# Decoder kernel on one core: the second half's first attention step placed between the steps of the first half's feed-forward

## The chip, the core and the metric

The kernel runs on one core of a Trainium2 chip. The metric is the device time of one launch in microseconds (us). TensorE multiplies matrices and transposes tiles through a matrix unit; VectorE, ScalarE and GpSimd work on tiles of 128 partitions; SyncE issues the DMAs. Each engine carries out its own list of instructions in the order written, and waits on semaphores for the others.

## What is computed

The input is 16 sequences of 128 tokens with 128 features. The reference, cut to its outline:

```python
x = x + encoder(layernorm(x))              # 4 layers: linear attention, ReLU feed-forward
x = x + cross_attention(layernorm(x), ctx) # 16 heads, softmax, mask
x = x + bit_ffn(layernorm(x))              # quantized products, 3-tap convolution, SiLU
x = x + topk_attention(layernorm(x))       # 16 heads, the 64 highest scores of each row
x = x + channel_attention(layernorm(x), ctx)
x = x + experts(layernorm(x))              # 8 experts, SiLU(x Wg) * (x Wu), Wd

# encoder, one layer; elu(t) + 1 is computed as relu(t) + min(exp(t), 1)
# at the start: x = sqrt(128) * x_in + position
h = layernorm(x) * s1 + b1
q, k, v = h @ Wq + bq, h @ Wk + bk, h @ Wv + bv
qp, kp = elu(q) + 1, elu(k) + 1
kv, ksum = kp.T @ v, sum(kp)               # per head
x = x + ((qp @ kv) / (qp @ ksum + eps)) @ Wo + bo
x = x + relu((layernorm(x) * s2 + b2) @ W1 + bf1) @ W2 + bf2
```

## The kernel before, in words

The 16 sequences are two halves of eight; a half is two slots (s = 0, 1) of four sequences, each slot a tile of 128 x 512 fp32. The first half runs alone: the encoder (`encode_half`, a loop of four layers), then `cross_and_forward(0)`: cross attention in eight turns, the quantized feed-forward ("bitnet") and the projections of the top-k attention. Then `beside_encoder` merges the first half's top-k attention (turn b = one sequence) with the second half's encoder: the encoder is eight steps, step k being layer k // 2 of slot k % 2, and turn b holds attention of step b + 1, feed-forward of step b, and the head of step b + 2. Then come `cross_and_forward(1)`, in whose gaps the channel attention and first experts of the first half run (`beside(n)`), and the second half's top-k turns with all the expert products.

The order of the work is written by hand in each engine's block; there is no planner. Semaphores count events: `both(s, n)` and `nth(s, n)` give the count at which the n-th event of a slot has happened, so an event that changes its place in the order needs another count.

What the change touches, by the lines of the kernel before:

- Layer norm on VectorE: `layer_norm` (1874: four statistics, four aggregates), GpSimd's `ln_rsqrt` (633) or `step_rsqrt` (818), then `normalize` (1886) or `step_normalize` (2263), four `tensor_scalar`. `ln(n, update)` (1911) does it for both slots around an update.
- The feed-forward, `cross_and_forward`. On VectorE (2453): after the cross attention's loop of ten passes `crossed` (2512) adds the residual (`residual`, 1943) and quantizes (`quantize`, 2495); then four chunks c of 128 hidden features (2536): scale the product (2543), maxima of the chunk before (2534), two tap sums per slot (2551, 2553); then the second quantization (2556), `convolved` (2573) with the last norm LN_D, and `topk_values` (2587: centering of the keys, values). On ScalarE (1208): copies, tap activations (1233), SiLU (1238), copies (1244), `projected` (960). On TensorE (1787): transposes of the quantized tile (1802), a product with ones (1805), products `first(c)` (1807), transposes of a chunk (1827), the second product (1829 to 1844), `topk_projections` (1310).
- Banks of PSUM of those products: `FORWARD_BANKS` and `PROJECT_BANKS` (101, 102). In the first half slot 0 has banks 0 to 3 and slot 1 has 4 to 7; in the second half they have 0, 1 and 2, 3.
- Between `cross_and_forward(0)` and turn -1: the second half's input norms (2605 to 2612), `embed(1)` (2238: sqrt(128) x + position, then the norm of step 0's and step 1's attention), `attend(0, "input")` and `"projections"` on TensorE (1603), "input", "queries", "keys" on ScalarE (1103), "projections" on VectorE (2367), `spread_keys(0)` on GpSimd (860).
- `attend(k, part)`, one step's attention in parts: TensorE 1485 ("input": transposes; "projections": 1498, 1502; "sums": 1507; "attention": 1513; "attended": transposes; "output": 1523), VectorE 2270 ("projections" 2278, 2279; "queries" 2282; "keys" 2286; "sums" 2289, 2290; "attention" 2294 to 2298; "output" 2303 with `step_norm`), ScalarE 1032.
- `merged_turn(b)` for b from -1 to 9 in each block. Turn -1 has attention of step 0 (all parts behind the projections), the scores of sequence 0 (`scores`, 1397; 1408), their copies and signs on ScalarE (973, 985), and the head of step 1.
- `residual_base` (691) on GpSimd adds the bias and the normed tile to the residual of the first half, two sums per slot, right after the norms LN_D.

```python
# VectorE, chunk c of the feed-forward (lines 2536 to 2555, cut)
for s in SL:
    dve.wait_ge(c_f1_mm, nth(s, hf * CH + c + 1))
    dve.tensor_tensor(cbuf[s][:, :, 1:P + 1], bank4(FORWARD_BANKS[hf][s][2]),
                      rsb[s][:, :].rearrange("p (b t) -> p b t", b=G), ALU.mult).then_inc(c_deq, 1)
if c >= 1:
    for s in SL:
        chunk_max(s, c - 1)
for s in SL:
    dve.wait_ge(c_tap1, nth(s, hf * CH + c + 1))
    ...
if hf == 1:
    beside(1)
```

Of the kernel before, what the change touches and what calls it, by code (L numbers as in the profile page):

```python
# [27 lines left out]
P = 128  # L28
NSEQ = 16
SLOTS = 2  # L30
G = 4
# [69 lines left out]
FORWARD_BANKS = (((0, 1, 2, 3, 0, 1, 2), (4, 5, 6, 7, 4, 5, 6)), ((0, 1, 0, 1, 0, 1, 0), (2, 3, 2, 3, 2, 3, 2)))  # L101
PROJECT_BANKS = (((0, 2, 1, 3), (4, 6, 5, 7)), ((0, 1, 0, 1), (2, 3, 2, 3)))
# [22 lines left out]
NORM_AT, TURNED_AT = enc_orders()  # L125
NX_AT = {}
# [76 lines left out]
def decoder(nc, x, ctx, mask, aw, acolA, acolB, arow, w2a, bw, bcol, brow, cw, cconv, dw, dcol, drow,  # L203
            erow, ecol, mg, mu, md, ident_d, const_d, pos_d, out):
    stack = ExitStack()
    with stack:
# [173 lines left out]

        def xbank(g, k):
            return bank4(k)[:, 0:GROUPS[g][1], :]
# [72 lines left out]

        def norm_no(kind, k):

            done = 2 * NLN + 2 + NORM_AT[kind, k] + 1
            return done, done - 4

        def turned_no(kind, k):
            return 2 * (2 * NTR + TURNED_AT[kind, k] + 1)
# [145 lines left out]
        def _(pool):  # L608
# [24 lines left out]
            def ln_rsqrt(s, n):  # L633

                pool.wait_ge(ln_var, nth(s, n + 1))
                met(pool)
                pool.tensor_scalar(veps[s][:, :], mv[s][:, :, 1], EPS, None, ALU.add).then_inc(ln_veps, 1)  # L637
                pool.wait_ge(ln_veps, nth(s, n + 1))
# [52 lines left out]
            def residual_base(s, hf):  # L691
# [3 lines left out]
                pool.wait_ge(ln_h, both(s, hf * NLN + (LN_D + 1)))  # L695
# [134 lines left out]
            def merged_turn(b):  # L830
# [17 lines left out]
                if 0 <= b + 1 < STEPS:  # L848
                    attend_base(b + 1)
                if 0 <= b < STEPS:  # L850
                    step_rsqrt("A", b + 2)
                if 0 <= b + 1 < STEPS:
                    step_rsqrt("F", b + 1)
                if 0 <= b < NB:
                    maxima_in_parts(b)

            def beside_encoder():
                for s in SL:
                    step_rsqrt("A", s)
                spread_keys(0)  # L860
                for b in range(-1, NB + 2):
# [32 lines left out]
            def cross_and_forward(hf):  # L894
# [5 lines left out]
                for s in SL:  # L900
                    ln_rsqrt(s, n0 + LN_C)
                for s in SL:
                    ln_rsqrt(s, n0 + LN_D)
                for s in SL:
                    residual_base(s, hf)
                if hf + 1 < HALVES:
                    for s in SL:
                        ln_rsqrt(s, n0 + (NLN + LN_IN))
# [14 lines left out]
        def _(act):  # L923
            def hT_copy(s, m, k):

                act.wait_ge(hT_mm, both(s, m + 1))
# [105 lines left out]
            def attend(k, part):  # L1032
                s, i = k % 2, L + k // 2
                if part == "input":
                    act.wait_ge(wqkv_in, i * 48 + 48)
                    act.wait_ge(hT_mm, turned_no("A", k))
                    act.activation(hT[s][:, :], bank(6), ACT.Identity, bias=colA[:, 1:2], scale=colA[:, 0:1]).then_inc(hT_done, 2)
                if part == "queries":
                    act.wait_ge(q_mm, both(s, i + 1))
                    act.activation(qe[s][:, :], bank(5), ACT.Exp, bias=colA[:, 2:3])  # L1040
                    act.activation(qT_of[1][s][:, :], bank(5), ACT.Relu, bias=colA[:, 2:3]).then_inc(q_exp, 2)
                if part == "keys":
                    act.wait_ge(k_raw, both(s, i + 1))
                    act.activation(ke[s][:, :, :], kk[s][:, :, :], ACT.Exp).then_inc(k_exp, 2)
                    act.activation(kp[s], kk[s][:, :, :], ACT.Relu).then_inc(k_relu, 2)
                if part == "attended":
                    act.wait_ge(atT_mm, both(s, i + 1))
                    act.copy(atT[s][:, :], bank(5)).then_inc(atT_done, 2)
# [1647 lines left out]
```

## Time and profile before

| | |
|---|---|
| runs, median (lowest to highest) | 1449.4 us (1447.85 to 1454.92), 3 runs |
| the profiled execution | 1452.73 us, span 1450.9 us |
| TensorE busy | 1053.8 us, 73% of the span |
| VectorE busy | 998.0 us, 69% |
| ScalarE busy | 671.1 us, 46% |
| GpSimd busy | 491.9 us, 34% |
| mean granted TensorE clock | 0.819 of full |
| chain that ended last | TensorE 49%, VectorE 28%, ScalarE 7%, GpSimd 7%, issue 7% |

The span is the time from the first to the last instruction; the execution's own time lies 1.8 us above it. Busy shares are averages over stages that have different limits, so they say little of a change in one stage: that is read from the timeline of the stage. The chain is followed back from the last instruction, at each step to what released it. The rows below are whole lines of such views; PE is TensorE, DVE VectorE, ACT ScalarE, POOL GpSimd; in square brackets stands the idle time before an instruction and what ended it.

### The profile page before, as it was taken

How to read it: one execution, taken by the hardware profiler on the slowest of the kernel's cores; microseconds unless marked ns; L12 is line 12 of the kernel's file. 1: busy time of each engine (PE TensorE's matmuls, PEld its weight loads, DVE VectorE, ACT ScalarE, POOL GpSimd, SP SyncE). 2: the span in 40 equal slices, each digit the busy share in tenths (PEclk: the TensorE clock that was granted, in tenths of full speed). 3: DMA queues.
4: the chain of work that ended last, by engine and by line, in shares of the span. 5: the costliest groups of instructions: out<-in, count | busy, mean ns of one | idle time of the engine just before them, and what ended most of it. 6: DMA issues, size and time to landing. Idle time of an engine off the chain costs nothing.

```text
span 1450.9 us, 17892 instructions
## 1 busy us (share of the span) xinstructions
PE 1053.8 (73%) x5079; PEld 695.7 (48%) x5082; DVE 998.0 (69%) x3100; ACT 671.1 (46%) x1767; POOL 491.9 (34%) x474
## 2 busy tenths in 40 slices
PE   2877775655476818777676669868899883888999
PEld 1766652323344515554454334433344462666887
DVE  5666657878637778778887886753776858765332
ACT  1443436733156526666423654325776653533322
POOL 5233235601335404444524730043343423331100
PEclk9898976765677767888655889989998986899999
DMA  3000110000000000000001001201111120223344
GB/s 124 21 18 29 29 41 9 1 0 1 0 10 21 12 3 17 14 17 9 1 1 51 1 1 37 66 22 47 52 45 45 48 73 15 67 77 92 113 135 123
DMA packets 41106, 53.88 MB, mean 37 GB/s; under 512 B 6112, under 2 KB 20080, under 8 KB 41008
## 3 DMA queue, kind: packets, MB, share of 16 engines
q1 hardware_dynamic: 40336, 50.80, 11.5%
q0 software_dynamic: 672, 1.98, 0.4%
q8 instruction: 37, 0.61, 0.2%
q14 instruction: 61, 0.50, 0.1%
HBM read 51.71 MB, written 1.05 MB: 36 GB/s over the span
## 4 chain that ended last, share of the span: by engine, by line
PE 49%; DVE 28%; ACT 7%; POOL 7%; issue 7%; DVEq 1%; DMA 0%; another core or an unknown queue 0%; SPq 0%; POOLq 0%; ACTq 0%
PE psum L1679 7%; PE psum L1690 6%; PE psum L1665 6%; PE psum L1450 2%; PE psum L1426 2%; PE psum L1757 2%; PE psum L1268 2%; PE psum L1346 2%; PE psum L1544 2%; DVE h L1890 2%; PE psum L1408 2%; PE psum L1764 2%; POOL Wk L680 2%; PE psum L1498 2%; ACT far L995 2%
## 5 line engine op out<-in xcount | busy, mean ns | idle before, releaser
L2188 DVE TENSOR_TENSOR big<-psum,qe 128x512 f32<-128x512 f32 x106 | 72.8, 687 | 154.7 <-PE psum L1690 75.4
L1144 ACT ACTIVATE qe<-psum 128x512 f32<-128x512 f32 x106 | 62.3, 596 | 124.4 <-PE psum L1679 120.3
L1665 PE MATMUL psum<-big,wexp 128*128 128x256 f32 (+1 forms) x340 | 115.8, 455 | 0.0
L995 ACT ACTIVATE far<-far,half_far,fmul 128x128 bf16<-128x128 bf16 x256 | 102.9, 488 | 22.7 <-DVE hit L1963 22.7
L637 POOL TENSOR_SCALAR veps<-mv 128x4 f32<-128x4 f32 x34 | 8.4, 246 | 294.6 <-DVE mv L1883 294.6
L1976 DVE MAX8 near<-Wk 128x8 f32<-128x128 f32 x512 | 103.0, 275 | 0.0
L1268 PE MATMUL psum<-ident,h 128*128 128x128 f32 x172 | 37.9, 347 | 78.4 <-DVE h L1890 53.3
L735 POOL TENSOR_TENSOR Wk<-Wk,far 128x1024 f32<-128x1024 f32 x32 | 68.2, 2136 | 67.9 <-ACT far L995 67.9
L1890 DVE TENSOR_SCALAR h<-xs,mv,rstd 128x128 f32<-128x128 f32 x128 | 57.9, 553 | 41.1 <-POOL rstd L639 37.9
L1665 PEld LDWEIGHTS psum<-big,wexp 128*128 128x128 f32 x340 | 69.0, 203 | 30.1 <-issue 21.9
L1346 PE MATMUL psum<-ident,Wk 128*128 128x128 f32 x256 | 48.0, 355 | 47.1 <-POOL Wk L680 44.2
L1690 PE MATMUL psum<-xin,wexp 128*128 128x512 f32 x128 | 70.4, 633 | 15.1 <-DVE far L2188 9.9
L973 ACT ACTIVATE S<-psum,tiny 128x1024 f32<-128x1024 f32 x32 | 35.7, 1114 | 92.3 <-PE psum L1408 92.3
L1679 PE MATMUL psum<-xin,wexp 128*128 128x512 f32 x128 | 76.0, 679 | 2.5 <-DVE vaug L2599 1.6
L985 ACT ACTIVATE far<-S 128x128 bf16<-128x128 f32 x256 | 75.0, 296 | 0.3
L726 POOL TENSOR_TENSOR Wk<-S,ngr 128x2048 f32<-128x2048 f32 x16 | 58.1, 3630 | 39.1 <-DVE hit L1963 39.1
L1346 PEld LDWEIGHTS psum<-ident,Wk 128*128 128x128 f32 x256 | 38.0, 182 | 69.0 <-POOL Wk L680 42.5
L1268 PEld LDWEIGHTS psum<-ident,h 128*128 128x128 f32 x172 | 23.5, 171 | 97.9 <-DVE h L1890 47.5
L757 POOL TENSOR_SCALAR nparts<-nmax 128x16 bf16<-128x16 f32 x16 | 5.2, 326 | 189.2 <-DVE nmax L2060 189.2
L1986 DVE MATCH_REPLACE8 Wk<-near,Wk 128x128 f32<-128x128 f32 x256 | 67.1, 273 | 0.0
L1426 PE MATMUL psum<-ctxT,kT 32*128 32x512 f32 x128 | 49.0, 848 | 23.4 <-DVEq L2054 22.2
L948 ACT ACTIVATE Wk<-S,nsm 128x128 f32<-128x128 f32 x128 | 49.5, 389 | 11.9 <-DVE nsm L2480 11.9
(343 smaller groups left out, 2915.0 us busy)
## 6 DMA issues: line engine op xcount, KB each, us to landing
wexp<-in_mg SPq DMA_DIRECT2D x48, 256.0 KB, 2.7
wexp<-in_mu SPq DMA_DIRECT2D x48, 256.0 KB, 3.0
wexp<-in_md SPq DMA_DIRECT2D x48, 256.0 KB, 3.0
w<-in_aw SPq DMA_DIRECT2D x8, 256.0 KB, 2.9
w<-in_w2a SPq DMA_DIRECT2D x8, 256.0 KB, 2.6
wqkv<-in_aw SPq DMA_DIRECT2D x8, 192.0 KB, 2.2
ctxt<-in_ctx SPq DMA_DIRECT2D x5, 256.0 KB, 4.6
xin<-in_x SPq DMA_DIRECT2D x4, 256.0 KB, 3.0
```

Source lines behind the costliest of these rows:

```text
L735: pool.tensor_tensor(Wk[t][:, heads, :], Wk[t][:, heads, :], far[t][:, heads, :], ALU.subtract).then_inc(z_ready, 1)
L985: ins = act.activation(far[n % 2][:, hd, :], S[n % 3][:, hd, :], ACT.Sign, accum_out=cnt[n % 2][:, hd:hd + 1])
L995: ins = act.activation(far[t][:, hd, :], far[t][:, hd, :], ACT.Identity, bias=half_far[:, 0:1], scale=fmul[t][:, hd:hd + 1])
L1268: mm = pe.transpose(dst[:, b * P:(b + 1) * P], src[:, b, :], eye)
L1346: mm = pe.transpose(bank(4 + g % 2)[:, j * P:(j + 1) * P], E[a % 2][:, 4 * g + j, :], ident[:, :])
L1426: pe.matmul(bank(j), kT_of[g // 2][g % 2][rows, c * P:(c + 1) * P], qblk[a % 2][rows, :, :].rearrange("p i q -> p (i q)"), start=True, sto ...
L1665: mm = pe.matmul(bank(4)[:, 0:w], wd[l % 2][:, c + j, :], hid_of[k >= EARLY][k % CH][:, j * w:(j + 1) * w], start=first and j == 0, stop=l ...
L1679: mm = pe.matmul(bank(5 + k % 2)[:, j * w:(j + 1) * w], wg[l % 2][:, (c + j) * P:(c + j + 1) * P], hTm[g], start=True, stop=True)
L1690: mm = pe.matmul(bank(U_BANK[k])[:, j * w:(j + 1) * w], wu[l % 2][:, (c + j) * P:(c + j + 1) * P], hTm[g], start=True, stop=True)
L1890: ins = dve.tensor_scalar(h[s][:, b, :], src[:, b, :], mv[s][:, b, 0:1], rstd[s][:, b:b + 1], ALU.subtract, ALU.mult)
L1976: ins = dve.max(near[:, hd, rank:rank + 8], Wk[t][:, hd, :])
L2188: dve.tensor_tensor(hid_of[k >= EARLY][k % CH], bank(U_BANK[k]), sg_of[k >= EARLY][k % 2], ALU.mult).then_inc(hu_done, 1)
```

## The change

Three things. First, order: the second half's input norms go into the last passes of the first half's cross attention; its embedding, the norm of step 0 and the whole attention of step 0 go between the steps of the first half's feed-forward, the output sum of step 0 and the statistics of step 1's norm between the two slots' `topk_values`. Turn -1 keeps the scores of sequence 0, the head of step 1, and the last normalization of both; `residual_base` goes there too. Second, tiles: what step 0 needs and the feed-forward still uses lies in parts of two score tiles, S[1] and S[2]. Third, banks: the first half's feed-forward uses four banks (0 to 3), as the second half's does, so that step 0 has banks 5 to 7. The counts of the moved events come from three tables.

```diff
-FORWARD_BANKS = (((0, 1, 2, 3, 0, 1, 2), (4, 5, 6, 7, 4, 5, 6)), ((0, 1, 0, 1, 0, 1, 0), (2, 3, 2, 3, 2, 3, 2)))
-PROJECT_BANKS = (((0, 2, 1, 3), (4, 6, 5, 7)), ((0, 1, 0, 1), (2, 3, 2, 3)))
+FORWARD_BANKS = (((0, 1, 0, 1, 0, 1, 0), (2, 3, 2, 3, 2, 3, 2)),) * HALVES
+PROJECT_BANKS = (((0, 1, 0, 1), (2, 3, 2, 3)),) * HALVES
...
+NORMS_MOVED = {e: 2 * LN_B + 3 + j for j, e in enumerate(
+    ((0, NLN + LN_IN), (1, NLN + LN_IN), (0, LN_C), (0, NLN + LN_A), (1, LN_C), (0, LN_D), (1, LN_D), (1, NLN + LN_A)))}
...
+        first_h = [S[1][:, 0:4, :], S[1][:, 4:8, :]]
+        first_kp, first_kk, first_ke = S[1][:, 8:12, :], S[2][:, 8:12, :], S[2][:, 12:16, :]
+        first_hT, first_qe = flat(S[2][:, 0:4, :]), flat(S[2][:, 4:8, :])
...
@@ GpSimd, merged_turn @@
-                if 0 <= b + 1 < STEPS:
+                if 1 <= b + 1 < STEPS:
                     attend_base(b + 1)
...
+                if b == -1:
+                    pool.wait_ge(ln_h, 2 * norm_no("F", 0)[0])
+                    for s in SL:
+                        residual_base(s, 0)
@@ GpSimd, beside_encoder @@
-                for s in SL:
-                    step_rsqrt("A", s)
                 spread_keys(0)
+                step_rsqrt("A", 1)
@@ GpSimd, cross_and_forward @@
+                if hf == 0:
+                    for s in SL:
+                        ln_rsqrt(s, NLN + LN_IN)
+                    ln_rsqrt(0, LN_C)
+                    ln_rsqrt(0, NLN + LN_A)
+                    ln_rsqrt(1, LN_C)
+                    pool.wait_ge(c_q1, 2)
+                    attend_base(0)
@@ ScalarE, cross_and_forward @@
                     act.activation(rsb[s][:, :], bank(FORWARD_BANKS[hf][s][1]), ACT.Copy, scale=wscale[:, 0:1]).then_inc(c_rs, 1)
+                    if hf == 0 and s == 0:
+                        attend(0, "input")
...
+                    if hf == 0 and c == 0:
+                        attend(0, "queries")
+                        attend(0, "keys")
                     for s in SL:
                         if hf == 1:
                             beside(1)
...
+                if hf == 0:
+                    attend(0, "attended")
@@ TensorE, topk_projections @@
-                if hf == 1:
-                    pe.wait_ge(pk_done, nth(s, 2 * hf + 2))
+                pe.wait_ge(pk_done, nth(s, 2 * hf + 2))
@@ TensorE, beside_encoder @@
-                attend(0, "input")
-                attend(0, "projections")
                 for b in range(-1, NB + 2):
                     merged_turn(b)
+                    if b == -1:
+                        projections_out(1, 0)
@@ TensorE, cross_and_forward: after the product with ones of slot 0; after chunk c; after slot 0's second product @@
+                    if hf == 0 and s == 0:
+                        attend(0, "input")
+                        attend(0, "projections")
...
+                    elif c >= 1:
+                        attend(0, ("sums", "attention", "attended")[c - 1])
...
+                    elif s == 0:
+                        attend(0, "output")
@@ VectorE, step_normalize @@
+                if (kind, k) in (("A", 2), ("F", 1)):
+                    dve.wait_ge(base_done, 4)
@@ VectorE, cross_and_forward @@
+                    if hf == 0 and b == NB:
+                        input_norm(0)
...
+                        if hf == 0:
+                            input_norm(1)
+                if hf == 0:
+                    for s in SL:
+                        normalize(s, NLN + LN_IN, xin[s], first_h[s])
...
                         quantize(0)
                         if hf == 1:
                             beside(1)
+                        else:
+                            embedded_first(0)
+                            dve.wait_ge(x_upd, sum_no(0, NLN + LN_A))
+                            layer_norm(0, NLN + LN_A, xs_of[1][0])
                     residual(hf, s)
+                    if hf == 0 and s == 1:
+                        normalize(0, NLN + LN_A, xs_of[1][0], first_h[0])
...
                 quantize(1)
                 if hf == 1:
                     beside(3)
+                else:
+                    embedded_first(1)
+                    attend(0, "projections")
...
                     if hf == 1:
                         beside(1)
+                    elif c == 0:
+                        attend(0, "keys")
+                        attend(0, "queries")
+                    elif c < CH - 1:
+                        attend(0, ("sums", "attention")[c - 1])
...
-                for s in SL:
-                    topk_values(s)
-                if hf + 1 < HALVES:
-                    for s in SL:
-                        dve.wait_ge(x_in[s], hf * 16 + 32)
-                        layer_norm(s, n0 + (NLN + LN_IN), xin[s])
-                    for s in SL:
-                        dve.wait_ge(base_done, 2 * nth(s, hf + 1))
-                        dve.wait_ge(hT_mm, both(s, hf * NTR + (TR_D + 1)))
-                        normalize(s, n0 + (NLN + LN_IN), xin[s])
+                topk_values(0)
+                if hf == 0:
+                    dve.wait_ge(x_upd, sum_no(1, NLN + LN_A))
+                    step_norm("A", 1)
+                    attend(0, "output")
+                topk_values(1)
...
+            def embedded_first(s):
+                dve.wait_ge(ln_h, 2 * ln_no(s, NLN + LN_IN))
+                dve.scalar_tensor_tensor(xs_of[1][s][:, :, :], first_h[s], float(np.sqrt(P)), pos[:, :].unsqueeze(1).to_broadcast([P, G, P]),
+                                         ALU.mult, ALU.add).then_inc(x_upd, 2)
```

In `attend` of each engine, `of_step(k, first, usual)` picks the tile in S[1] or S[2] for step 0 and the slot's own tile otherwise, and step 0's pair of banks for "sums" and "attention" is 6, 7 instead of 3, 4. `merged_turn` starts its attention at step 1 (`step = 1 <= b + 1 < STEPS`).

## Rows read from the trace of the kernel before

**Rows 1.** Windows: us; PE, PEld, DVE, ACT, POOL busy; PEclk; DMA
```profile
299.00:370.00 71.00, 37.18 (x170) 21.33 (x169) 59.18 (x153) 22.96 (x36) 10.64 (x12) 0.62 0.00 0
...
370.00:402.00 32.00, 13.72 (x44) 10.38 (x46) 17.65 (x60) 4.95 (x7) 8.33 (x11) 0.60 0.00 1
...
402.00:423.00 21.00, 11.72 (x34) 6.61 (x35) 10.31 (x24) 12.94 (x46) 7.22 (x5) 0.66 0.05 16
...
560.00:600.00 40.00, 31.98 (x180) 22.48 (x180) 31.22 (x131) 25.15 (x73) 17.54 (x17) 0.83 0.08 24
```

**Rows 2.** Timeline of TensorE (PE): start, us, line, operation, [idle before]
```profile
330.10 1.11 PE L1268 MATMUL psum<-ident,kk 128*128 128x128 f32 x4 [0.34 <-DVE kk L2553]
...
367.45 1.05 PE L1287 MATMUL psum<-watt,hT 128*128 128x128 f32 x8
...
380.36 1.09 PE L1268 MATMUL psum<-ident,h 128*128 128x128 f32 x4 [11.85 <-DVE h L1890]
...
382.49 3.75 PE L1498 MATMUL psum<-wqkv,hT 128*128 128x256 f32 x8 [1.04 <-ACT hT L1037]
...
386.03 1.41 PE L1502 MATMUL psum<-hT,wqkv 128*128 128x512 f32 x2
...
390.65 2.10 PE L1507 MATMUL psum<-vv,big 128*128 128x130 f32 x8 [3.22 <-DVE big L2286]
...
393.76 2.26 PE L1513 MATMUL psum<-kvs,qT 128*128 128x144 f32 x8 [1.00 <-DVE kvs L2290]
...
399.80 2.04 PE L1523 MATMUL psum<-wo,hT 128*128 128x128 f32 x8 [0.82 <-ACT hT L1048]
...
401.77 2.08 PE L1408 MATMUL psum<-kblk,qT 32*128 32x512 f32 x4
...
434.25 1.13 PE L1408 MATMUL psum<-kblk,qT 32*128 32x512 f32 x4
```

**Rows 3.** Timeline of VectorE (DVE), first attention of the second half
```profile
387.28 0.68 DVE L2278 TENSOR_TENSOR kk<-psum,rowkv 128x512 f32<-128x512 f32 x1
...
392.80 0.69 DVE L2289 TENSOR_TENSOR kvs<-psum,consts 128x512 f32<-128x512 f32 x1 [1.59 <-PE psum L1507]
...
396.13 0.23 DVE L2294 TENSOR_SCALAR den<-psum 128x64 f32<-128x64 f32 x1 [2.51 <-PE psum L1513]
...
414.61 0.69 DVE L2278 TENSOR_TENSOR kk<-psum,rowkv 128x512 f32<-128x512 f32 x1 [7.86 <-PE psum L1498]
```

**Rows 4.** Timeline of VectorE, first half from the cross attention's end on
```profile
289.47 1.22 DVE L1929 TENSOR_REDUCE zden<-Wk 128x8 f32<-128x1024 f32 x1 [1.18 <-ACT Wk L951]
...
296.44 0.69 DVE L1938 TENSOR_TENSOR far<-psum,consts 128x512 f32<-128x512 f32 x1 [1.64 <-PE psum L1357]
...
299.77 0.69 DVE L1947 TENSOR_TENSOR xs<-psum,xb 128x512 f32<-128x512 f32 x1 [1.55 <-PE psum L1364]
...
319.95 1.29 DVE L2543 TENSOR_TENSOR cbuf<-psum,ke 128x512 f32<-128x512 f32 x2 [2.94 <-remote]
...
361.04 3.15 DVE L1890 TENSOR_SCALAR h<-xs,mv,rstd 128x128 f32<-128x128 f32 x4 [1.58 <-POOL rstd L639]
```

**Rows 5.** Timeline of VectorE, embedding norm of the second half
```profile
376.05 0.87 DVE L1878 BATCH_NORM_STATS2 stats<-xs 128x6 f32<-128x128 f32 x4
...
379.10 1.11 DVE L1890 TENSOR_SCALAR h<-xs,mv,rstd 128x128 f32<-128x128 f32 x4 [1.65 <-POOL rstd L824]
```

**Rows 6.** Timeline of ScalarE (ACT), around a table load
```profile
1055.20 1.28 ACT L1004 ACT_TABLE_LOAD   x1
...
1056.50 1.02 ACT L1004 ACTIVATE big<-psum 128x1024 f32<-128x1024 f32 x1
```

**Rows 7.** Timeline of GpSimd (POOL), the first residual sum
```profile
360.97 1.27 POOL L696 TENSOR_TENSOR xs<-xs,ratt 128x512 f32<-128x512 f32 x1
```

**Rows 8.** Windows of five us around the stretch without TensorE work
```profile
365.00:370.00 5.00, 2.88 (x12) 1.73 (x12) 4.46 (x14) 1.95 (x3) 2.33 (x2) 1.00 0.00 0
...
380.00:385.00 5.00, 3.60 (x10) 2.81 (x11) 3.24 (x12) 2.06 (x2) 2.48 (x4) 0.50 0.00 0
```

More of the change, by code:

```diff
@@ L454, in cols, with ln_no, sum_no, tr_no @@
             return slice(WU * (u % 2), WU * (u % 2 + 1))
+        def ln_no(s, n):
+            return NORMS_MOVED[s, n] if isinstance(n, int) and (s, n) in NORMS_MOVED else nth(s, n + 1)
+        def sum_no(s, n):
+            return SUMS_MOVED[s, n] if isinstance(n, int) and (s, n) in SUMS_MOVED else both(s, n - n // NLN)
+        def tr_no(s, m):
+            return TURNED_MOVED[s, m] if (s, m) in TURNED_MOVED else both(s, m + 1)
         def norm_no(kind, k):
             done = 2 * NLN + 2 + NORM_AT[kind, k] + 1
-            return done, done - 4
+            return NORMS_MOVED[0, NLN + LN_A] if (kind, k) == ("A", 0) else done, done - 4
         def turned_no(kind, k):
-            return 2 * (2 * NTR + TURNED_AT[kind, k] + 1)
+            return TURNED_MOVED["A", 0] if (kind, k) == ("A", 0) else 2 * (2 * NTR + TURNED_AT[kind, k] + 1)
         def up_no(k, c):
@@ L1102, in beside_encoder @@
             def beside_encoder():
-                for part in ("input", "queries", "keys"):
-                    attend(0, part)
                 for b in range(-1, NB + 2):
@@ L1490, in attend @@
                     if k == 1:
-                        pe.wait_ge(v_raw, both(0, i + 1))
-                    transposes(bank(6), h[s], ident[:, :], hT_mm, 2)
+                        pe.wait_ge(lin_done, both(0, i + 1))
+                    transposes(bank(6), h_of("A", k), ident[:, :], hT_mm, 2)
                 if part == "projections":
@@ L1555, in merged_turn @@
                 before, old, new = 0 <= b - 1 < NB, 0 <= b - 2 < NB, 0 <= b + 1 < NB
-                step, fed, after = 0 <= b + 1 < STEPS, 0 <= b < STEPS, 0 <= b + 2 < STEPS
+                step, fed, after = 1 <= b + 1 < STEPS, 0 <= b < STEPS, 0 <= b + 2 < STEPS
                 if b == 7:
@@ L2316, in merged_turn @@
                 here, before, old = 0 <= b < NB, 0 <= b - 1 < NB, 0 <= b - 2 < NB
-                step, fed, after = 0 <= b + 1 < STEPS, 0 <= b < STEPS, 0 <= b + 2 < STEPS
+                step, fed, after = 1 <= b + 1 < STEPS, 0 <= b < STEPS, 0 <= b + 2 < STEPS
                 if b == 7:
```

98 lines of the change are left out of this document (56 added, 42 removed).

## Prediction

> **What bounds the kernel now.** I read the stretches first [rows 1]: between 370 and 402 us TensorE works 13.72 of 32 us and VectorE 17.65, ScalarE 4.95; nobody is busy, so this stretch is a chain. The timelines show which: input norm, embedding norm, then attention step 0, each waiting on the one before. TensorE sat idle 11.85 us before the first transposes [rows 2], and VectorE waits 1.59 and 2.51 us for the first products [rows 3]. The stretch ahead, 299 to 370 us, is different: VectorE is busy 59.18 of 71 us, TensorE 37.18 [rows 1]; it is VectorE's. The change takes work out of a chain with little overlap and lays it into a stage that VectorE bounds. The question is what each laid-in part costs there, including the waits it makes VectorE stand through, for VectorE, ScalarE and TensorE all run their own list in order.
>
> A difference under 0.5% (7 us) is about what a measurement of this kernel cannot tell from no change.
>
> **What the edits cost inside the first half's tail.** All of it is counted as the delay of the last normalization of the half (slot 1, start 361.04 [rows 4]).
>
> 1. Input norms. Slot 0's statistics (about 1.4 us) go ahead of a sum that had waited 1.18 us for ScalarE, slot 1's into the 1.64 us that VectorE idles for TensorE's outputs [rows 4]: nothing, or 0.1. Without those two covers they cost 2.8. The two normalizations (4 x 0.28 us each, 2.2 together) get the 1.55 idle before the cross attention's residual sum [rows 4]: **+0.6**.
> 2. Behind slot 0's quantization come embedding 0 (0.7, as the other sums over 512 [rows 3]), its statistics (1.4), and its normalization (1.11). That last waits for GpSimd's rstd: from the start of the statistics to the normalization the same pattern takes 3.05 us [rows 5], that is 1.64 of waiting, of which slot 1's residual sum fills 0.7. So 0.7 + 1.4 + 0.9 + 1.1 = **+4.1**. GpSimd's five rsqrts stand in VectorE's new order, so none waits behind another.
> 3. TensorE gets slot 0's transposes and projections ahead of slot 1's quantized transposes. They take 1.09 + 3.75 + 1.4 us with a ScalarE copy of 0.8 between [rows 2], about 7.1 us from the end of embedding 0's normalization; VectorE needs 8.0 us from there: 3.05 and 1.1 for slot 1's norm [rows 5], 3.85 for its quantization, which ended 2.94 before 319.95 [rows 4]. So TensorE is free in time. VectorE's embedding 1 and two projection sums (0.68 each [rows 3]) are 2.0 us, and VectorE had those 2.94 us of idle before the first chunk: **0**. GpSimd's sum for the attention's base (1.3 us) runs beside them. Without this cover it would be 2; a faster TensorE may give back up to 0.9 of the idle.
> 4. After chunk 0: keys and queries, two sums of 0.68, need the ScalarE exponentials, which now stand behind the chunk's two tap activations and take 2.3 us; that adds 0.15 of waiting. The Silu's table load (1.28 us [rows 6]) now comes after them, and Silu and the next taps land 0.7 us before VectorE wants them: **+1.5**.
> 5. After chunk 1: "sums" on VectorE directly waits for TensorE, whose products stand behind the transposes of the chunk just ended (the pair takes 1.0 us to the next issue; slot 1's own start at 330.10 [rows 2]) and take 2.10 at the low clock, about half at the high one. Nothing is between: VectorE stands 3.1 us (low) or 2.2 (high), then works 0.8. **+3.5** (3.0 to 3.9).
> 6. After chunk 2: "attention" in the same way, transposes and then 2.26 us of products [rows 2]: stands 3.3 or 2.2, then 1.7 us (two small ones and one of 0.7). **+4.5** (3.9 to 5.0). Queued behind both waits are the next chunk's scaling and maxima, and behind them ScalarE's taps and TensorE's next transposes: the whole stage shifts.
> 7. TensorE's "output" (2.04 us [rows 2]) stands between slot 0's second product and slot 1's transposes, which were ready the moment that product ended, and slot 1's product met VectorE with 0.1 us to spare: **+1.4** (0.9 to 1.9).
> 8. Four banks: the banks are reused, and each reuse already has a wait that has ended by then; the one new wait (values for the keys' copy) 0 to 0.1 us.
>
> Sum: 0.6 + 4.1 + 0 + 1.5 + 3.5 + 4.5 + 1.4 = **15.6 us later** (13.1 to 16.9).
>
> **What it takes out behind that normalization.** Before, from its start (361.04) to the second slot's projection sums (414.61 [rows 3]) 53.6 us pass. After:
> - the normalization no longer has GpSimd's residual sums beside it: it took 3.15 us for four that take 1.11 elsewhere [rows 4, 5], while GpSimd ran its sum at 360.97 [rows 7]. Those sums are now in turn -1, where VectorE has little to do. The normalization then frees slot 1's transposes at about +1.2, but TensorE is at slot 0's values until +2.7.
> - slot 1's tail on TensorE runs from the normalization's end (361.04 + 3.15 [rows 4]) to 368.50 (its last products [rows 2]), 4.3 us, and the scores of turn -1 follow at once, at +7.1. Their spread keys need 1.1 us of GpSimd behind slot 0's centering and are early.
> - from the scores to the projection sums is 12.84 us at the low clock (401.77 to 414.61), 11.0 in turn 0, where the scores take 1.13 instead of 2.08 [rows 2]. I take 12: +19.1.
> - on VectorE in that time: values 0 (2.3), norm of embedding 1 (1.4), output sum and norm (2.1), values 1 (2.3, after TensorE), two normalizations (2.2): done at about +11.6, when slot 1's transposes can go; TensorE is ready for them at about +10.5 to +11. It fits, with up to 1 us lost in the bound.
> - GpSimd's four base sums (1.27 us each [rows 7]) then end near +17, before the signed scores of turn 0 are asked for (+21). No new DMA is issued; SyncE's weight loads wait for the same events, earlier.
>
> 53.6 - 19.1 = **34.5 us** (30.9 if slot 1's tail and the scores all run at the low clock, which adds 2.8 to the tail; 35.5 at the high one).
>
> Net 34.5 - 15.6 = **18.9 us less**. The profiled execution took 1452.7 us around its span of 1450.9, so it would be 1433.8; the median of the runs is 3.3 lower, 1449.4, and I give the forecast against that: **1430.5**. All terms at the low clock: 30.9 - 16.9 = 14.0; all at the high one: 35.5 - 13.1 = 22.4.
>
> **Two rules of the skill.** Behind the table load at 1055.20 (1.28 us) the Exp starts at 1056.50 [rows 6], so a load costs 1.3 us here. The Trainium skill, ScalarE: Activation LUTs, section "What ACT_TABLE_LOAD costs", has a drain of about as much again on each switch, 2.66 us in all. By that, point 4 would be 0.6 us dearer, 1.4 less 0.7 to spare; the trace does not show it.
> The clock was 0.50 of full from 380 to 385 us, after TensorE had done nothing for 10 us, and 1.00 from 365 to 370 us, after steady work [rows 8]. The Trainium skill, TensorE: Matmul & The Clock Gate, "What's actually happening", says that idling halves the clock and sustained work restores it. By that, the filled hole should leave turn -1 at 2.4 GHz; the trace agrees at those two places, and over the feed-forward stage, with TensorE at work on and off, it was 0.62 [rows 1].
>
> **The rivals.**
> - *Clock stays high* (10%): the hole was what halved the clock, and turn -1 and the inserted products all run at 2.4 GHz. Gain 22.4 and up to 4 more if the next turn's start profits: 1423 to 1427. For it: 0.66 in 402 to 423 against 0.83 in a later turn [rows 1]. Against: that later turn still has its drops.
> - *More standing than I see* (12%): VectorE, in order, meets waits I sized at nothing (points 1 and 3 uncovered, 4.8; slot 1's transposes late in turn -1, 2): gain 8 to 14, 1437 to 1441.
> - *Serial all the same* (6%, no difference): every inserted part costs its full chain, so the 32 us of 370 to 402 are all paid in the feed-forward stage, and only GpSimd's interference (2.0) and slot 1's tail beside the new work (3.3) are saved: 1444. For it: points 5 and 6 are of that kind. Against: projections, copies and exponentials, some 12 us of the chain, run beside VectorE's work; 11.85 of TensorE's idle is gone anyway.
> - *Slower* (4%): the clock of the merged turns. A turn of 40 us has TensorE busy 32 at clock 0.83 [rows 1]; about half of the chain is TensorE's, 19 us. Should the shifted start put its drops on the chain, each turn costs 19 x (0.83/c - 1): at 0.71 it is 3.2 us, 26 over eight turns, which is the point where 19 us of gain turn into 7 of loss; at 0.68 it is 34, 1464. Against: the turns' order of work is unchanged.
>
> Forecast 68%. Faster 90% (forecast, high clock, more standing), same 6%, slower 4%. The range takes all of the forecast's span, most of the high-clock case and most of the standing case: 1422 to 1440.
>
> **What would show it.** VectorE waits of 2.2 to 3.1 us before the masked sums and 2.2 to 3.3 before the denominators, now ahead of the last normalization; that normalization 15.6 us later and 1.1 us long for its four; the 11.85 us hole gone; scores of turn -1 some 18 us earlier; turn 0 and all after it merely shifted. Wrong if turns 0 to 7 change length by more than 1 us each, if the first chunk starts late, or if the scores wait for spread keys or for slot 0's values.

## The result and the profile after

The changed kernel takes 1426.61 us (median of 4 runs, 1424.53 to 1429.59), the kernel before in the same comparison 1450.77 us: ratio 0.9835, interval 0.9807 to 0.9864, about 24 us less. The forecast was 18.9 us less, 1430.5. The profiled execution took 1429.59 us around a span of 1427.8. Line numbers of the changed kernel differ: 1890 is now 1947, 1947 is 2004, 2543 is 2620, 1408 is 1451, 1843 is 1893, 1523 is 1567, 2278 is 2339.

Two executions do not reach the changed code at the same time, so the sections below are counted from an anchor that both kernels have ahead of the first changed instruction, a reduction of the cross attention (before, then after, VectorE's timelines):

```profile
267.81 1.21 DVE L1929 TENSOR_REDUCE zden<-Wk 128x8 f32<-128x1024 f32 x1
```
```profile
266.13 1.21 DVE L1986 TENSOR_REDUCE zden<-Wk 128x8 f32<-128x1024 f32 x1
```

1.68 us of the difference between the two spans is therefore there before anything is changed. The stretches of [rows 1] in the kernel after (windows, same columns):

```profile
299.00:370.00 71.00, 37.20 (x169) 25.55 (x170) 57.40 (x151) 22.86 (x36) 6.72 (x9) 0.62 0.00 0
370.00:402.00 32.00, 21.01 (x71) 12.09 (x72) 19.48 (x65) 18.57 (x55) 18.09 (x15) 0.79 0.04 11
402.00:423.00 21.00, 15.78 (x76) 10.59 (x76) 8.84 (x32) 14.08 (x50) 8.18 (x7) 0.84 0.02 7
```

The windows are fixed times, and the feed-forward stage now runs until 373 us (before: 361), so they do not hold the same code. VectorE is busy 57.40 of 71 us instead of 59.18, although attention work was laid into the stage: it now stands in new waits, which the timeline below shows. The chain of 370 to 402 is gone (TensorE 13.72 to 21.01 us busy, ScalarE 4.95 to 18.57). VectorE's timeline, which answers to [rows 3 to 5]:

```profile
299.29 0.68 DVE L2004 TENSOR_TENSOR xs<-psum,xb 128x512 f32<-128x512 f32 x1
...
311.55 1.11 DVE L1947 TENSOR_SCALAR S<-xs,mv,rstd 128x128 f32<-128x128 f32 x4 [1.01 <-POOL rstd L668]
...
322.23 1.28 DVE L2620 TENSOR_TENSOR cbuf<-psum,ke 128x512 f32<-128x512 f32 x2
328.00 1.28 DVE L2620 TENSOR_TENSOR cbuf<-psum,ke 128x512 f32<-128x512 f32 x2
336.30 0.69 DVE L2351 TENSOR_TENSOR kvs<-psum,consts 128x512 f32<-128x512 f32 x1 [2.94 <-PE psum L1551]
...
337.04 1.28 DVE L2620 TENSOR_TENSOR cbuf<-psum,ke 128x512 f32<-128x512 f32 x2
345.60 0.22 DVE L2356 TENSOR_SCALAR den<-psum 128x64 f32<-128x64 f32 x1 [3.20 <-PE psum L1557]
...
347.19 1.28 DVE L2620 TENSOR_TENSOR cbuf<-psum,ke 128x512 f32<-128x512 f32 x2
368.95 1.13 DVE L2662 SCALAR_TENSOR_TENSOR xs<-psum,deq,xs 128x128 f32<-128x128 f32 x4 [0.51 <-PE psum L1893]
...
373.09 1.11 DVE L1947 TENSOR_SCALAR h<-xs,mv,rstd 128x128 f32<-128x128 f32 x4 [1.58 <-POOL rstd L668]
...
389.85 0.69 DVE L2339 TENSOR_TENSOR kk<-psum,rowkv 128x512 f32<-128x512 f32 x1 [5.68 <-PE psum L1542]
```

The first chunk no longer has idle time ahead of it (2.94 us in the kernel before). The four chunks start at 322.23, 328.00, 337.04 and 347.19, that is 5.77, 9.04 and 10.15 us apart. Ahead of the third and fourth stand the forecast waits, 2.94 before the masked sums and 3.20 before the denominators; both sit in front of the next chunk's scaling in VectorE's list. The last normalization takes 1.11 us for its four, as forecast. TensorE's timeline from the last second products on, with [rows 2] for before:

```profile
361.26 1.89 PE L1893 MATMUL psum<-wcq,big 128*128 128x128 bf16 x16 [0.68 <-ACT big L1288]
362.95 2.02 PE L1567 MATMUL psum<-wo,S 128*128 128x128 f32 x8
...
367.85 1.07 PE L1893 MATMUL psum<-wcq,big 128*128 128x128 bf16 x16 [0.72 <-ACT big L1288]
...
374.25 0.66 PE L1312 MATMUL psum<-ident,h 128*128 128x128 f32 x4 [1.11 <-DVE h L1947]
...
378.63 1.13 PE L1451 MATMUL psum<-kblk,qT 32*128 32x512 f32 x4
...
383.20 0.66 PE L1312 MATMUL psum<-ident,S 128*128 128x128 f32 x4 [1.00 <-DVE S L2328]
```

The same product of sixteen takes 1.89 us in slot 0 and 1.07 in slot 1: between the two, the clock rose. It stayed up over slot 1's tail and the scores (windows of the kernel after, columns as in [rows 1]):

```profile
345.00:363.00 18.00, 7.44 (x48) 5.62 (x46) 16.32 (x35) 5.45 (x9) 0.00 (x0) 0.50 0.01 1
363.00:368.00 5.00, 4.03 (x29) 3.34 (x28) 3.24 (x16) 2.15 (x4) 1.27 (x2) 0.60 0.00 0
368.00:373.00 5.00, 4.27 (x32) 2.76 (x30) 2.82 (x14) 1.96 (x3) 1.22 (x2) 1.00 0.00 0
373.00:378.00 5.00, 3.16 (x14) 1.55 (x13) 4.70 (x20) 1.61 (x3) 1.09 (x2) 1.00 0.00 2
378.00:383.00 5.00, 2.89 (x15) 1.14 (x13) 4.75 (x20) 2.23 (x3) 4.04 (x5) 1.00 0.02 3
383.00:390.00 7.00, 4.70 (x13) 3.62 (x14) 1.32 (x6) 6.95 (x35) 5.02 (x4) 0.57 0.00 0
```

So TensorE had 2.4 GHz from 368 to 383, and 1.2 GHz from 345 to 363, where it was at work for 7.44 of 18 us. The Trainium skill, TensorE: Matmul & The Clock Gate, section "What's actually happening", has sustained work bring the full clock and idling take it away. The rise agrees: it came behind 363 to 368 us, where TensorE was at work for 4.03 of 5 us. The fall agrees less well: the clock is 1.00 from 383 to 384 us and 0.51 from 384 to 385, so it fell although TensorE had been idle no longer than 1.31 us at a time since it rose.

Behind that the turns are shifted almost unchanged. A maximum of turn 0 moved from 446.49 to 422.71 us, 23.78 us earlier; the same maximum of each later turn comes 23.08 to 23.43 us earlier, and the first masking of the second cross attention moved from 782.20 to 758.93 (before, then after, VectorE's timeline):

```profile
446.49 2.28 DVE L2060 TENSOR_REDUCE nmax<-S 128x16 f32<-128x2048 f32 x1
...
782.20 2.44 DVE L2473 COPY_PREDICATED S<-maskt,psum 128x2048 f32<-128x2048 int32 x1 [2.65 <-PE psum L1334]
```
```profile
422.71 2.28 DVE L2117 TENSOR_REDUCE nmax<-S 128x16 f32<-128x2048 f32 x1
...
758.93 2.44 DVE L2534 COPY_PREDICATED S<-maskt,psum 128x2048 f32<-128x2048 int32 x1 [2.65 <-PE psum L1377]
```

The books of the two profiled executions, in us: upstream -1.68; last normalization later by 13.73 (from the anchor 106.96 against 93.23); from it to the second slot's projection sums 16.76 instead of 53.57, so -36.81; at those sums -24.76 in all; given back behind them 1.66, of which 0.98 by the maximum of turn 0; spans -23.1.

### The profile page after: what moved, and what is told of

It is laid out like the page before. It is cut to its first block, busy times and chain, and to the rows that moved or that the text cites. A ratio compares the mean times of both kernels' runs of the same rounds, so it can differ in the third digit from the quotient of the medians.

```text
span 1427.8 us, 17894 instructions
## 1 busy us (share of the span) xinstructions
PE 1048.4 (73%) x5079; PEld 693.7 (49%) x5082; DVE 990.6 (69%) x3100; ACT 670.7 (47%) x1767; POOL 492.4 (34%) x474
## 4 chain that ended last, share of the span: by engine, by line
PE 49%; DVE 28%; ACT 8%; issue 7%; POOL 6%; DVEq 1%; DMA 0%; SPq 0%; POOLq 0%; ACTq 0%
PE psum L1724 7%; PE psum L1735 6%; PE psum L1710 6%; PE psum L1493 2%; PE psum L1802 2%; PE psum L1469 2%; PE psum L1588 2%; PE psum L1312 2%; PE psum L1809 2%; PE psum L1451 2%; PE psum L1389 2%; POOL Wk L709 2%; DVE h L1947 2%; ACT far L1034 2%; PE psum L1542 2%
## 5 line engine op out<-in xcount | busy, mean ns | idle before, releaser
L1312 PE MATMUL psum<-ident,h 128*128 128x128 f32 x160 | 34.4, 342 | 67.0 <-DVE h L1947 41.8
L1947 DVE TENSOR_SCALAR h<-xs,mv,rstd 128x128 f32<-128x128 f32 x120 | 51.2, 530 | 37.9 <-POOL rstd L668 37.9
```

What stands on the lines that cost most here:

```text
L1312: mm = pe.transpose(dst[:, b * P:(b + 1) * P], src[:, b, :], eye)
L1947: ins = dve.tensor_scalar(to[:, b, :], src[:, b, :], mv[s][:, b, 0:1], rstd[s][:, b:b + 1], ALU.subtract, ALU.mult)
```

## The experiments

All ratios are against the kernel before on the same chip. The first four ran together (before: 1452.73 us, median of 11), the last four together (1454.21, of 23). Since executions differ by some us in parts that no edit touches, the sections of the edited stage are compared. They come from one execution of each kernel; where the code is the same and the clock too, they repeat closely (C to N of before, e1 and e6: 41.09, 41.09, 41.10). In the table, in us, from each execution's own trace: A the anchor; R the residual sum of slot 0 (299.77 in [rows 4]); C the first chunk's scaling; N the last normalization; K the first scores; P the second slot's projection sums.

| kernel | ratio, interval | A to R | R to C | C to N | N to K | K to P | R to P |
|---|---|---|---|---|---|---|---|
| before | 1 | 31.96 | 20.18 | 41.09 | 40.73 | 12.84 | 114.84 |
| after | 0.9835, 0.9807 to 0.9864 | 33.16 | 22.94 | 50.86 | 5.54 | 11.22 | 90.56 |
| e1 norms only | 0.9911, 0.9887 to 0.9934 | 32.36 | 24.21 | 41.09 | 24.59 | 13.11 | 103.00 |
| e2 attention back | 0.9862, 0.9839 to 0.9884 | 32.35 | 23.09 | 42.15 | 15.56 | 13.01 | 93.81 |
| e3 late waits | 0.9774, 0.9751 to 0.9797 | 31.98 | 22.95 | 45.52 | 5.55 | 11.22 | 85.24 |
| e4 sums behind the norm | 0.9857, 0.9832 to 0.9881 | 33.16 | 22.95 | 50.88 | 8.80 | 11.22 | 93.85 |
| e5 output late | 0.9819, 0.9793 to 0.9846 | 32.36 | 23.07 | 50.00 | 8.23 | 11.22 | 92.52 |
| e6 banks only | 1.0003, 0.9985 to 1.0022 | 31.77 | 20.19 | 41.10 | 40.28 | 13.11 | 114.68 |
| e7 product put in | 1.0007, 0.9987 to 1.0026 | 31.79 | 20.19 | 41.69 | 42.71 | 12.78 | 117.37 |
| e8 output before slot 1's product | 0.9775, 0.9751 to 0.9799 | 33.16 | 22.95 | 45.53 | 5.54 | 11.09 | 85.11 |

**e1, norms only.** The input norms and the embedding with its norm stay moved, as do the banks and the residual sums; all of step 0's attention goes back behind the feed-forward.

The edit, abridged:

```diff
@@ TensorE, ScalarE, VectorE, cross_and_forward @@
-attend(0, ...)              # every part
@@ TensorE, ScalarE, VectorE, beside_encoder and merged_turn @@
+attend(0, ...)              # as in the kernel before
```

> The changed kernel with the whole attention of step 0 (from its transposes on) back in turn -1; the input norms, the embedding and step 0's norm stay in the first half's tail. Theory A (the gain is overlap, part by part): the tail's last normalization 3.5 us later than before (after: 12.5 later), but the chain from step 0's transposes to the second projection sums, 34 us, stands again behind it, starting about 6 us after that normalization: some 8 us under the kernel before, 1442 us, so two thirds of the gain are the attention's. Theory B (most of the gain is the norms' chain and GpSimd's interference, the attention gives back what it takes): 15 us or more under before, 1435 or less. On the clock: if step 0's transposes and projections are what raised TensorE's clock at 320 us, chunk 0 starts about 1.2 us later here, counted from the end of slot 1's quantization; if they are not, it starts as early.

Measured 1440.11 us, 12.6 less than before. R to C grew by 4.03, near the 4.1 of step 2 of the prediction. The second slot's embedding sum, 0.7 us of step 3, lies in the same stretch and was covered: VectorE's idle time ahead of the first chunk went from 2.94 to 2.34 us. C to N is that of before to 0.01. Here TensorE's product with ones ran at half clock, and VectorE still idled ahead of the first chunk (VectorE's timeline of e1, then TensorE's of e1, then of after):

```profile
322.22 1.29 DVE L2610 TENSOR_TENSOR cbuf<-psum,ke 128x512 f32<-128x512 f32 x2 [2.34 <-remote]
```
```profile
319.73 2.02 PE L1847 MATMUL psum<-kk,ones 128*128 128x512 f32 x2
```
```profile
320.81 1.08 PE L1850 MATMUL psum<-kk,ones 128*128 128x512 f32 x2
```

With the projections ahead of it (after) the same product took 1.08, and R to C was 1.27 shorter with more work in it. The expectation had forecast 1.2 us if the projections raise the clock, and no difference if they don't. So the projections are not only free there, they give back a little over 1 us. About half of the whole gain comes from the norms, with GpSimd's sums moved (11.8 of 24.3 in R to P).

**e2, attention back.** Transposes, projections, exponentials, keys and queries stay in the feed-forward; sums, attention, transposes and output go back to turn -1.

The edit, abridged (ScalarE's "attended" goes back too):

```diff
@@ TensorE, after chunk c; after slot 0's second product @@
-elif c >= 1:
-    attend(0, ("sums", "attention", "attended")[c - 1])
...
-elif s == 0:
-    attend(0, "output")
@@ VectorE, after chunk c; behind step_norm("A", 1) @@
-elif c < CH - 1:
-    attend(0, ("sums", "attention")[c - 1])
...
-attend(0, "output")
```

> The changed kernel with sums, attention, attended and output of step 0 back in turn -1; transposes, projections, keys and queries stay in the feed-forward. Theory A: turn -1 gets 11.1 us of chain back (390.65 to 401.77 of before), the feed-forward loses waits and work of 3.5 + 4.6 + 0.3: 2.7 us over the changed kernel, 1429. Theory C (clock: the inserted products, above all output between the two slots' second products, brought TensorE to full rate by 367 us): the clock in the 5 us before the last normalization is again 0.5, slot 1's tail takes its low-clock time, and the kernel is 5 us or more over the changed one, 1432.

Measured 1433.01 us; its interval overlaps that of after (0.9839 to 0.9884 against 0.9807 to 0.9864), so the totals hardly tell them apart. In the sections, C to N is 42.15, +1.06 over before: keys and queries. R to P is 93.81 against 90.56: the four parts that the change lays into the feed-forward bring 3.3 us only, for they cost 8.7 in C to N (50.86 - 42.15) and save 11.8 behind N. From 378 us on TensorE ran at 1.2 GHz (windows of e2):

```profile
378.00:391.00 13.00, 8.97 (x23) 4.68 (x22) 4.06 (x17) 7.92 (x36) 6.44 (x6) 0.50 0.00 0
```

The scores took 2.08 us each there and 1.13 in the kernel after, twice 0.95, about the 1.8 us between 13.01 and 11.22 in K to P.

**e3, late waits.** VectorE takes the masked sums and the attention one chunk later in its list, behind the next chunk's scaling and maxima. TensorE's list is that of after.

```diff
 if c >= 1:
     for s in SL:
         chunk_max(s, c - 1)
+if hf == 0 and c >= 2:
+    attend(0, ("sums", "attention")[c - 2])
...
-elif c < CH - 1:
-    attend(0, ("sums", "attention")[c - 1])
```

> The changed kernel with VectorE's sums and attention parts of step 0 moved behind the next chunk's scaling and maxima (2.55 us of work) instead of ahead of them. Theory A (the two waits of 2.94 and 3.20 us are pure standing, VectorE bounds the stage): both shrink to under 0.7 us, the last normalization comes 5 us earlier, 1421.5 us. Rival (the waits only move: ScalarE's taps and TensorE's transposes are then what VectorE waits for): 0 to 2 us gained.

Measured 1420.58 us, with e8 the lowest ratio of all; its interval lies clear below that of after. VectorE's timeline of e3:

```profile
334.85 0.69 DVE L2351 TENSOR_TENSOR kvs<-psum,consts 128x512 f32<-128x512 f32 x1 [0.42 <-PE psum L1551]
...
341.22 0.23 DVE L2356 TENSOR_SCALAR den<-psum 128x64 f32<-128x64 f32 x1 [0.27 <-PE psum L1557]
```

The waits fell from 2.94 and 3.20 to 0.42 and 0.27, 5.45 together; C to N fell by 5.34 and R to P by 5.32. What VectorE stood was on the path, all but 0.1 us, and nothing up to the projection sums took it back. The rival, that the waits only move to the taps and transposes, forecast a gain of 0 to 2 us and is out.

**e4, sums behind the norm.** GpSimd's residual sums go back to where they were, right after the norms LN_D.

```diff
@@ GpSimd, merged_turn @@
-if b == -1:
-    pool.wait_ge(ln_h, 2 * norm_no("F", 0)[0])
-    for s in SL:
-        residual_base(s, 0)
@@ GpSimd, cross_and_forward @@
-if hf == 1:
-    for s in SL:
-        residual_base(s, hf)
+for s in SL:
+    residual_base(s, hf)
```

> The changed kernel with GpSimd's four residual sums back right behind the first half's last norms. Theory A (they stretched VectorE's last normalization from 1.1 to 3.15 us and would hold up the spread keys): normalization 2 us longer, scores of turn -1 about 2.5 us later, 1429. Rival (their place is free): no difference, 1426.5.

Measured 1430.88 us, an interval that overlaps that of after. Up to N it is the kernel after to 0.02 us; N to K is 3.26 longer. VectorE's, GpSimd's and TensorE's timelines of e4:

```profile
368.16 3.13 DVE L1942 TENSOR_SCALAR h<-xs,mv,rstd 128x128 f32<-128x128 f32 x4 [1.58 <-POOL rstd L668]
```
```profile
368.10 1.26 POOL L725 TENSOR_TENSOR xs<-xs,ratt 128x512 f32<-128x512 f32 x1
```
```profile
371.35 0.66 PE L1307 MATMUL psum<-ident,h 128*128 128x128 f32 x4 [3.12 <-DVE h L1942]
372.73 2.08 PE L1319 MATMUL psum<-hT,watt 128*128 128x512 f32 x2 [0.73 <-ACT hT L961]
```

The four normalizations beside GpSimd's two sums take 3.13 us instead of 1.11. The Trainium skill, GPSIMD Engine Reference, section "Specifications" (row "SBUF interfaces"), says that GpSimd shares these with VectorE; no run here isolates the port, but the 2.0 us follow the placement of the sums. The other 1.2 us lie in TensorE's tail: it now idled 3.12 us instead of 1.11, the clock fell, and the first of slot 1's projections took 2.08 us, the second 1.54 (in the kernel after 1.13 and 1.02).

**e5, output late.** TensorE's output of step 0 goes from between the two second products to behind slot 0's projections of the top-k attention.

```diff
 for s in SL:
     topk_projections(s, hf)
+    if hf == 0 and s == 0:
+        attend(0, "output")
```

> The changed kernel with TensorE's output of step 0 between the two slots' top-k projections (where TensorE had idled 1.11 us) instead of between the two slots' second products. Theory C (the output's products, filling TensorE's time from 362.95 on, are what brings the clock to full by 367 us): slot 1's second product is again at half rate (1.9 us), slot 0's values end about 2 us after the last normalization starts instead of with it, and the scores of turn -1 start at +7.5 instead of +5.5: net 1 to 1.5 us slower, 1428. Theory O (order alone): the 0.51 us wait before slot 1's sum goes, the output fits in the idle time: 0.5 us faster, 1426.

Measured 1430.10 us, ratio 0.9819; the interval overlaps that of after, so the totals don't tell them apart. The sections do: chunk 3 to N is 25.30 us against 25.90 of after (0.6 less), N to K 2.69 longer. TensorE's timeline of e5:

```profile
364.63 1.07 PE L1893 MATMUL psum<-wcq,big 128*128 128x128 bf16 x16 [0.70 <-ACT big L1288]
...
368.20 2.08 PE L1324 MATMUL psum<-hT,watt 128*128 128x512 f32 x2 [0.73 <-ACT hT L966]
...
373.49 1.31 PE L1567 MATMUL psum<-wo,S 128*128 128x128 f32 x8
```

Slot 1's second product was at full rate here too, without the output ahead of it. So the output is not what raised the clock in the kernel after, as one theory of the expectation had it. In e2, which has neither the output nor the sums and the attention in the feed-forward, that product took 1.89. But then the clock fell, and slot 0's projections took 2.08, 1.91 and 1.92 us where the kernel after has 1.12, 1.02 and 1.16: 2.6 us more, about the 2.7 of N to K. The output itself takes 1.31 us there, and the 1.11 us that TensorE idled at that place are gone. In these two executions the kernel with the output ahead of slot 1's product kept the full clock longer; that the output's place is the cause is not shown.

**e6, banks only.** The kernel before with the four banks and the wait that they need.

```diff
-FORWARD_BANKS = (((0, 1, 2, 3, 0, 1, 2), (4, 5, 6, 7, 4, 5, 6)), ((0, 1, 0, 1, 0, 1, 0), (2, 3, 2, 3, 2, 3, 2)))
+FORWARD_BANKS = (((0, 1, 0, 1, 0, 1, 0), (2, 3, 2, 3, 2, 3, 2)),) * HALVES
...
-if hf == 1:
-    pe.wait_ge(pk_done, nth(s, 2 * hf + 2))
+pe.wait_ge(pk_done, nth(s, 2 * hf + 2))
```

> The kernel before with the four banks and the added wait alone. All theories: 0 to +0.1 us, no difference from before; the chunks at the same distances as before. If the reuse of banks cost something, chunk 0 or the values would come later.

Measured 1.0003, interval 0.9985 to 1.0022; C to N 41.10 against 41.09. The reuse of banks costs nothing that shows.

**e7, a product put in.** The kernel before with one fp32 product of 512 columns (two matmul records) between the second products, its result used by nothing: the kernel computes all that it did, and this besides.

```diff
+elif s == 0:
+    pe.matmul(bank(3), watt[0][:, 3 * P:4 * P], watt[1][:, :], start=True, stop=True)
```

> The kernel before with one more product of 128 x 512 on TensorE, of no use, between slot 0's and slot 1's second product of the first half (2 us at half rate, where the change puts the output). Theory C: the clock is 1.00 by the time of slot 1's second product (1.1 us instead of 1.89) and slot 0's values end before the last normalization starts; VectorE waits 0.5 us before slot 1's sum. As the last normalization is stretched by GpSimd here, the scores don't profit: the time is that of before, within 1 us. Rival: clock still 0.50 there, slot 1's sum waits 1.8 us, time up by that.

Measured 1.0007, interval 0.9987 to 1.0026. TensorE's timeline of e7:

```profile
347.14 2.02 PE L1848 MATMUL psum<-watt 128*128 128x512 f32 x2
...
352.04 1.07 PE L1843 MATMUL psum<-wcq,big 128*128 128x128 bf16 x16 [0.89 <-ACT big L1244]
...
360.48 0.66 PE L1268 MATMUL psum<-ident,h 128*128 128x128 f32 x4 [3.32 <-DVE h L1892]
361.87 2.08 PE L1280 MATMUL psum<-hT,watt 128*128 128x512 f32 x2 [0.73 <-ACT hT L927]
```

2.02 us of added work made C to N only 0.60 longer; slot 1's second product then ran in 1.07 instead of 1.89 us. But TensorE idled 3.32 us at the slow last normalization, the clock fell, slot 1's projections ran at half rate, and R to P ended 2.5 us longer than before; in the total that does not show. In this execution the added work came with an earlier rise of the clock, which was lost again behind the idle time.

**e8, output before slot 1's product.** e3, with the output behind slot 1's transposes, in the time in which TensorE waits for ScalarE's copy.

```diff
+if hf == 0 and s == 1:
+    attend(0, "output")
...
-elif s == 0:
-    attend(0, "output")
```

> The kernel with the late waits, and TensorE's output of step 0 between slot 1's transposes and its second product, where TensorE waits 0.7 us for ScalarE's copy, instead of ahead of the transposes. Order alone: 0.3 to 0.5 us less waiting before slot 1's sum, 1420. If the clock rises later by that, slot 1's product and the tail give it back: 0 to +1.

Measured 1422.59 us, 0.9775: the same as e3 (0.9774), and C to N is 45.53 against 45.52. That equality is partly luck. In e3 VectorE waited 0.47 us before slot 1's sum, and in e8 it does not wait there at all, as expected; but e8 waited 0.68 us instead of 0.27 before the denominators, ahead of the edited place, where TensorE's transposes took 1.12 us instead of 0.66. VectorE's timelines of e3, then of e8, and TensorE's of e3, then of e8:

```profile
362.16 1.13 DVE L2662 SCALAR_TENSOR_TENSOR xs<-psum,deq,xs 128x128 f32<-128x128 f32 x4 [0.47 <-PE psum L1893]
```
```profile
342.76 0.23 DVE L2356 TENSOR_SCALAR den<-psum 128x64 f32<-128x64 f32 x1 [0.68 <-PE psum L1557]
...
363.14 1.13 DVE L2662 SCALAR_TENSOR_TENSOR xs<-psum,deq,xs 128x128 f32<-128x128 f32 x4
```
```profile
338.62 0.66 PE L1312 MATMUL psum<-ident,kk 128*128 128x128 f32 x4 [0.79 <-DVE kk L2632]
```
```profile
339.61 1.12 PE L1312 MATMUL psum<-ident,kk 128*128 128x128 f32 x4 [0.79 <-DVE kk L2632]
```

So the new place takes 0.47 us of waiting away in the stage; whether the whole kernel gains by it, these runs do not show.

## Why the prediction was right, and where its sizes were off

The direction, the chain that goes, and the two waits that come were as forecast. The sum was 18.9; from the anchor to the projection sums the change brought 23.1, 4.2 more. That is also more than the 22.4 that the prediction gave with all terms at the high clock: the cost, 13.73, lies within its 13.1 to 16.9, but the saving, 36.81, lies above its 35.5, since that bound kept the 7.1 us from the normalization to the scores. By the prediction's steps, from the two profiled executions:

| step | forecast | measured | where |
|---|---|---|---|
| 1 input norms | +0.6 | +1.20 | A to R |
| 2, 3 embedding, projections | +4.1, 0 | +2.76 | R to C |
| 4 keys and queries | +1.5 | +1.29 | chunk 0 to 1, 5.77 against 4.48 |
| 5 sums | +3.5 | +3.51 | chunk 1 to 2, 9.04 against 5.53 |
| 6 attention | +4.5 | +4.63 | chunk 2 to 3, 10.15 against 5.52 |
| 7 output | +1.4 | +0.34 | chunk 3 to N, 25.90 against 25.56 |
| sum | 15.6 | 13.73 | |
| normalization to scores | 7.1 | 5.54 | N to K |
| scores to sums | 12 | 11.22 | K to P |
| saved behind the normalization | 34.5 | 36.81 | N to P |

- **Step 1** named the right edit, but one number was too sure. Counted from a later reduction, the last but one of the cross attention and still ahead of the first changed instruction of VectorE, the way to R takes 14.59 us before and 14.61 in e6. It takes 14.98 or 14.99 in e1, e2, e3 and e5, and 16.02 to 16.05 in after, e4 and e8, all with the same code there: 0.4 or 1.4 us. The granted clock up to the next such reduction was 0.80 or 0.81 in the first group and 0.50 in the second. So the cost goes with the clock that the code ahead left behind; no run sets that clock on purpose. The reduction (before, then after, VectorE's timelines):

```profile
285.18 1.21 DVE L1929 TENSOR_REDUCE zden<-Wk 128x8 f32<-128x1024 f32 x1
```
```profile
283.25 1.21 DVE L1986 TENSOR_REDUCE zden<-Wk 128x8 f32<-128x1024 f32 x1
```
- **Step 2** was right: e1 gives 4.03 with the covered embedding sum. **Step 3** took 0 and left up to 0.9 as possible; the two steps together measured 2.76, 1.3 below the sum of their terms, and in the kernel after the product with ones ran at the full clock (1.08 against 2.02 us in e1). The step's cover held.
- **Step 4** had a table load in it. ScalarE's timeline of the kernel after:

```profile
326.67 1.28 ACT L1280 ACT_TABLE_LOAD   x1
327.96 1.08 ACT L1280 ACTIVATE big<-psum 128x512 f32<-128x512 f32 x2
```

The Silu starts 1.29 us after the load does. The drain of the Trainium skill's page ScalarE: Activation LUTs, section "What ACT_TABLE_LOAD costs", does not show on this switch either. What the prediction would have added by it (1.4 less 0.7, which is 0.7 and not its 0.6) did not come.
- **Steps 5 and 6** were right to 0.13 us, and e3 shows their cause: when VectorE meets the same products one chunk later, 5.34 of the 8.14 us are gone. The rest is the work itself and the 0.69 us of waiting that e3 keeps.
- **Step 7** failed as the prediction put it. The product did stand in front of slot 1's transposes, but the term took slot 1's second product at 1.89 us. It ran in 1.07, and VectorE waited 0.51 at slot 1's sum: +0.34 instead of +1.4. e7 shows the same with another product (+0.60 for 2.02 us of work).
- **Step 8** was right (e6).
- **Behind the normalization** the terms took TensorE's clock as partly low: 12 us from scores to sums between 12.84 and 11.0, and slot 0's values in the way of slot 1's transposes until +2.7. The clock was 1.00 from 368 us, those values were done as the normalization started, and the scores came at +5.54. The two terms make the whole 2.3 us. The 2.0 us of GpSimd's interference were sized right (e4: 3.13 against 1.11).

So what was mis-sized, in four places, is TensorE's clock; for step 1 this rests on the two groups of runs alone. The rival "clock stays high" forecast 1423 to 1427, and the measured time lies in that range, but only half of its mechanism came: turn -1 ran at 2.4 GHz until 383 us, while the products of steps 5 and 6 took 1.94 and 2.13 us, near the 2.10 and 2.26 of [rows 2], and the granted clock was 0.50 from 342 to 363. Against the rival "serial all the same" speaks e2: exponentials, projections and keys cost 1.06 us in C to N and nothing in R to C. The rival "more standing" (whose gain of 8 to 14 would give 1435 to 1441, not 1437) did not come: no idle time stood ahead of the first chunk, and slot 1's transposes in turn -1 waited 1.00 us at 383.20. The slower rival did not come: from the projection sums to the end of the execution 1.66 us were given back, far from 26, and from one turn's maximum to the next the two kernels differ by 0.70 us at most.

The gain is smaller than the hole that was filled because the sums, the attention and the output, as placed, cost in the feed-forward nearly all that they save behind it: 3.3 us are left (after against e2). With VectorE's waits moved by one chunk (e3 against e2) 8.6 us are left, and the kernel is faster than both: 1420.58 us.

## What to carry to other kernels

Work laid into a stage that another engine bounds costs what that engine stands in waits: put the consumer behind the next independent piece of its own list, not right behind the producer's issue (e3, 5.3 us for two moved lines). Sum such a change by sections from an anchor ahead of the first changed instruction. Price every product on a chain at both clocks, and look in the trace for where the high one is lost behind it.

## What the runs showed of the hardware

- Added TensorE work can cost less than its duration: 2.02 us of product made the path to the last normalization 0.60 longer (e7), and projections ahead of a product made the stretch 1.27 shorter than without them (after against e1). The full clock did not last in both: it fell behind an idle stretch of 3.32 us (e7) and 3.12 (e4), and was kept over one of 1.11 (after). In e5 it fell with idle stretches no longer than 1.04 us, and in the kernel after, at 384 us, with none longer than 1.31, so idle time alone does not tell; what else decides stays open.
- VectorE's four normalizations of 128x128 take 1.11 us alone and 3.13 beside two GpSimd sums of 128x512; the two sums beside them take 1.26 each (e4), as they do in turn -1 of the kernel after (1.26 and 1.27).
- Kernels that are the same up to there reached the anchor between 261.17 us (e4) and 267.81 (before), and from the projection sums to the end of the span the executions took 1036.3 (before) to 1041.2 us (e4). Why was not tried.
